# Causal attention, second pass: triangles masked by GpSimd zero writes in place of TensorE mask products

## What is computed

```
q, k, v = proj(Wq), proj(Wk), proj(Wv)
sim = einsum('bhid,bhjd->bhij', q, k) / sqrt(hd)
sim = where(triu(ones((n, n)), k=1), neg, sim)
beta = function of the entropy of softmax(sim), one number per row
attn = softmax(sim * beta)
out = einsum('bhij,bhjd->bhid', attn, v) @ Wo.T + bo
```

## Time and profile before

| | us |
|---|---|
| median of 3 runs | 2211.95 (2209.3 to 2216.09) |
| profiled execution, its own time | 2228.5 |
| its span in the trace | 2226.7 |
| PE, DVE, ACT, POOL busy in it | 1622.6, 1482.7, 1396.0, 141.3 |
| mean granted TensorE clock | 0.753 |

### The profile page before, as it was taken

The page is one execution under the profiler, slowest core; times in us unless marked ns, Lnnn a source line. Parts: engine busy times, 40 slices in busy tenths (PEclk is TensorE's granted clock), DMA queues, the critical chain, the costliest instruction groups (busy, mean ns, idle before and its releaser), DMA issues. The chain is left out here.

```text
span 2226.7 us, 22386 instructions
## 1 busy us (share of the span) xinstructions
PE 1622.6 (73%) x6402; PEld 690.0 (31%) x6402; DVE 1482.7 (67%) x3509; ACT 1396.0 (63%) x2635; POOL 141.3 (6%) x126
## 2 busy tenths in 40 slices
PE   4786899999999643777778787788787877511166
PEld 2343344444444201232223332232222333201144
DVE  6645354535463799888887788877878763479922
ACT  4464443434333598989989999899999986300012
POOL 0000000000000100000000000000000000035364
PEclk9898899999999755676765667656655578755578
DMA  4000065554556201111111011110101002240031
GB/s 147 0 0 0 16 160 156 132 155 128 158 147 168 68 34 33 55 47 61 38 47 46 29 58 41 44 46 31 58 29 37 36 24 87 58 123 0 0 104 48
DMA packets 56668, 147.37 MB, mean 66 GB/s; under 512 B 7760, under 2 KB 22480, under 8 KB 53936
## 3 DMA queue, kind: packets, MB, share of 16 engines
q1 hardware_dynamic: 52320, 136.63, 20.6%
q0 software_dynamic: 3072, 8.39, 1.3%
q10 hardware_dynamic: 1152, 0.92, 0.3%
HBM read 126.38 MB, written 19.53 MB: 66 GB/s over the span
## 5 line engine op out<-in xcount | busy, mean ns | idle before, releaser
L1712 DVE CUSTOM_DVE_ANT_0 sa_e<-sa_ps,sa_mask 128x1024 f32<-128x1024 f32 (+7 forms) x512 | 385.9, 754 | 107.0 <-PE sa_ps L1459 101.5
L1459 PE MATMUL sa_ps<-sa_space 72*128 72x512 bf16 (+3 forms) x768 | 296.9, 456 | 188.2 <-DVE sa_nmax L1712 140.1
L1721 DVE CUSTOM_DVE_ANT_0 sa_lg<-sa_e,sa_lg 128x1024 f32<-128x1024 f32 (+7 forms) x512 | 386.4, 755 | 67.3 <-ACT sa_lg L1612 67.0
L1602 ACT ACTIVATE sa_e<-sa_e,sa_nmax 128x1024 f32<-128x1024 f32 (+7 forms) x512 | 406.6, 794 | 20.1 <-DVE sa_nmax L1712 19.4
L1612 ACT ACTIVATE sa_lg<-sa_e,sa_sum 128x1024 f32<-128x1024 f32 (+7 forms) x512 | 405.5, 792 | 5.0 <-DVE sa_prod L1721 4.7
L1620 ACT ACTIVATE sa_p<-sa_ps 128x512 f32<-128x512 f32 x576 | 338.4, 610 | 71.6 <-PE sa_ps L1509 40.7
L1509 PE MATMUL sa_ps<-sa_q2s,sa_k2s 75*128 75x512 bf16 (+3 forms) x768 | 297.7, 432 | 50.1 <-ACT sa_p L1620 35.9
L974 DVE TENSOR_TENSOR mx_hw<-mx_spread,mx_h 128x512 f32<-128x512 f32 x256 | 176.1, 691 | 232.2 <-PE mx_ps L813 197.1
L875 ACT ACTIVATE mx_h<-mx_ps 128x512 f32<-128x512 f32 (+1 forms) x264 | 157.0, 597 | 276.6 <-PE mx_ps L800 256.0
L800 PE MATMUL mx_ps<-mx_f,m 128*128 128x512 f32 x512 | 261.4, 596 | 0.8 <-ACT mx_h L875 0.8
L813 PE MATMUL mx_ps<-mx_hw,m 128*128 128x512 f32 x512 | 259.8, 594 | 1.0 <-DVE mx_hw L974 1.0
(11 more groups left out here) (322 smaller groups left out, 1846.2 us busy)
## 6 DMA issues: line engine op xcount, KB each, us to landing
mx_spread<-mx_spill SPq DMA_DIRECT2D x256, 256.0 KB, 4.0
sa_space<-sa_spill_q SPq DMA_DIRECT2D x96, 96.0 KB
sa_space<-sa_spill_k SPq DMA_DIRECT2D x96, 96.0 KB
sa_k2s<-sa_spill_k SPq DMA_DIRECT2D x48, 192.0 KB
sa_q2s<-sa_spill_q SPq DMA_DIRECT2D x48, 192.0 KB
m<-m_in SPq DMA_DIRECT2D x1, 4256.0 KB, 18.5
records<-sa_e SPq DMA_DIRECT2D x8, 512.0 KB, 5.3
be_w<-w_in SPq DMA_DIRECT2D x16, 256.0 KB, 11.4
```

Of the source, the lines that this page charges most:

```text
L1459: last = nc.tensor.matmul(out[:, col:col + w], q_ring[:, c % 2, local, i * P:(i + 1) * P], k_ring[:, c % 2, local, col:col + w], start=Tru ...
L1602: nc.scalar.activation(e[:, u % 5, 0:w], e[:, u % 5, 0:w], ACT.Exp, scale=-1.0, bias=nmax[:, b % 2, i, h:h + 1], accum_out=sums[:, b % 2, ...
L1712: nc.vector.tensor_tensor_reduce(out=e[:, u % 5, 0:w], in0=slot_of("unit", u)[:, 0:w], in1=mask_wide[:, SEQ - w:SEQ], scale=1.0, scalar=3. ...
L1721: nc.vector.tensor_tensor_reduce(out=lg[:, u % 2, 0:w], in0=e[:, u % 5, 0:w], in1=lg[:, u % 2, 0:w], scale=1.0, scalar=0.0, op0=ALU.mult, ...
```

## The change

The mask products of the second pass (L1512) are left out: PE computes the diagonal blocks unmasked, and ACT exponentiates them as they are. POOL then goes through the packs: for each diagonal block it waits until all four exponentials of the pack are done, and one `affine_select` over 128 partitions x 4 heads x 128 columns of fp32 in `p_t`, in place, keeps an element where column >= partition and writes 0.0 elsewhere. `answer(v)` gets one more wait, on POOL's count up to and including pack v. There is one `affine_select` for a single pack and two for a double pack, 128 in all, and 512 fewer products on PE. The mask of the first pass (`mask_wide`) stays.

```diff
+        def own_cols(s):
+            return [sum(w for _, _, w in PACKS[s][:k]) for k, (j, q, _) in enumerate(PACKS[s]) if q == j * P]
+
+        def own_blocks(v):
+            g, s = divmod(v, NPACKS)
+            return TILES * g + sum(len(own_cols(k)) for k in range(s))
+
+        masked = sig("sa_masked")
+
...
             def _(pool):
                 pool.wait_ge(mask_ready.sem, 2)
                 nc.gpsimd.memset(k2_ring[64:ROWS2, :, :, :], 1.0).then_inc(ready.sem, 1)
+                for v in range(ALL2):
+                    for col in own_cols(v % NPACKS):
+                        pool.wait_ge(exp2_ready.sem, GROUP * (v + 1))
+                        whole = p_t[:, v % 2, :, col:col + P]
+                        nc.gpsimd.affine_select(out=whole, in_=whole, pattern=[[0, GROUP], [1, P]], compare_op=ALU.is_ge,
+                                                fill=0.0, base=0, channel_multiplier=-1
+                                                ).then_inc(masked.sem, 1)
...
                     for j, q, w in PACKS[s]:
-                        own = q == j * P
                         last = nc.tensor.matmul(out[:, col:col + w], k2_ring[:, g % 2, hh, j * P:(j + 1) * P],
-                                                q2_ring[:, g % 2, hh, q:q + w], start=True, stop=not own)
-                        if own:
-                            last = nc.tensor.matmul(out[:, col:col + P], ident_b[:, :], mask_k,
-                                                    start=False, stop=True)
+                                                q2_ring[:, g % 2, hh, q:q + w], start=True, stop=True)
                         col += w
                     last.then_inc(s2_mm.sem, 1)
...
                     pe.wait_ge(exp2_ready.sem, GROUP * (v + 1))
+                    if own_blocks(v + 1):
+                        pe.wait_ge(masked.sem, own_blocks(v + 1))
```

## The result

The changed kernel takes 2223.46 us (median of 7 runs, 2218.88 to 2228.5) against 2212.38 for the kernel before (7 runs, 2206.95 to 2217.06) beside it: a ratio of 1.0052, 95% interval 1.004 to 1.0065. It is slower by 11 us. The profiled execution took 2223.03 us, with a span of 2221.3 and a mean granted clock of 0.735.

A forecast was written before the change was run, and what follows sets the result against it. ACT was taken to set the main stage's pace, with PE leading in the tail. The terms -3 - 4 + 6 + 3 + 8 = +10 us, on the median of 2211.95, gave 2222 us; range 2200 to 2262.

The forecast's parts named there:

- Masks out, main stage and tail: PE without 512 mask products: main stage -3 us (bounds 0 and -42), tail -4 us (bounds 0 and -5).
- ACT's waits fall in packs 6 and 7: Sign to look for: ACT's waits before its second-pass exponential should fall in these packs and rise in the tail.
- Ended with a mask product: ACT's waits for PE where a mask product was the last thing awaited: 12.6 us main stage, 18.4 us tail.
- The select's duration: POOL's time per 128x512 select, taken as 1.5 us from a one-input TENSOR_SCALAR; two with hand-over 3.2 us.
- The wait in the main stage: Double packs' answers wait for POOL beyond their slack; PE late by 22 us, a quarter let through: +6 us.
- the 2.5 us of slack: Main stage: time from a double pack's last exponential to its answer, which hides POOL's selects up to that length.
- The expected 0.5 to 1 us for packs 1 and 8: Sign to look for: the answer's new wait on POOL in these main-stage packs.
- DVE and POOL side by side: Main stage: selects hold off DVE's two-input product, 13 us of DVE time, a quarter let through: +3 us.
- The tail: Answers with almost no slack wait for POOL; PE late by 16.5 us, half let through: +8 us.
- the 104 to 110 us named: Sign to look for: the tail's length after the change, instead of 101 us.
- The fast select rival: Selects below 1.15 us each, no main-stage overrun, PE relieved: -12 us, 2200 us; chance 0.20.
- The reading, 0.62 of 1.49 us: From the earlier trace: a one-input POOL operation holds DVE's two-input ones off only for its first 0.62 us.

The follow-up runs named there:

- the second measurement: The changed kernel itself, unaltered, timed once more beside the kernel before: 1.0036.
- the kernel with neither: Changed kernel without mask products, selects or the wait on POOL; triangles unmasked, second-pass exponentials at 1/128 of their scale: 0.9954 of the kernel before.
- Selects aside: Changed kernel without mask products; the 128 selects run on a tile of their own, no answer waits; exponentials at 1/128 scale: 1.0008 of the kernel before.
- memsets aside: As Selects aside, but each select is a memset of the same size, so POOL writes and reads nothing: 0.9974 of the kernel before.

## Why the prediction was right, and which step failed

The forecast was 2222 us; the median is 2223.46. The sum of +10 stands against +11 measured (1.0052; 1.0036 in the second measurement is +8), and it is made of terms that did not all hold.

- **Masks out, main stage and tail (-3 and -4).** Measured together as -10, by the kernel with neither. The bounds of 0 to -47 held it. In the last 21 packs of the tail they show as nothing (85.8 us with masks, 86.5 without), so the split into -3 and -4 isn't borne out. The expectation that ACT's waits fall in packs 6 and 7 did not come true: read from the gaps on ACT, pack 6 has 8.0 us instead of 8.4 and pack 7 has 6.6 in both. "Ended with a mask product" was no measure of what the wait would lose.
- **The select's duration (1.5 us): this is the step that failed.** A select takes 0.63 us when DVE lets it, and 0.82 on the mean, from 0.63 up to 1.62. I had taken the TENSOR_SCALAR as the nearest row because inputs and output agree. The memset at 530 ns was the nearer one.
- **The wait in the main stage (+6): nil.** With 0.63 to 0.82 us a double pack's two selects fit into the 2.5 us of slack; of 67 masked packs three answers waited, for 0.7 us in all. The expected 0.5 to 1 us for packs 1 and 8 did not come. The slack of the double packs was read rightly. That of single packs was not: 3.9 us holds for pack 0, but pack 6 has 1.2 to 2.4 us in 8 of its 13 answers. With selects of 0.63 us nothing came of it.
- **DVE and POOL side by side (+3): mis-sized.** Selects aside cost 0.54% over neither on the same chip, 12 us. The sum counted 13 us of DVE's time, a quarter of which was to reach the end; DVE's busy time grew by 4.7 us only, since `product` rose by 6 ns and not by 30. So the time held was put too high and its effect too low. The hold also goes both ways, and the sum counted one of them: POOL is held too, by 24 us in all (128 x 0.19), with single selects at up to 1.62 us.
- **The tail (+8, with -4 of masks): right in size, by another sum.** +4 forecast net, +4.9 and +4.5 in two profiles, inside the 104 to 110 us named; the last answer waited 2.24 us for POOL. Without the first two packs, where the kernel before had the lower clock by chance, it is +7.1 to +7.5. The overrun was smaller than I had summed (9.0 us against 16.5). The rest came from what I had put at 0 here: the selects' presence beside DVE and a clock of 0.83 instead of 0.86. Selects that nobody waits for cost 4 to 6 us in the last 21 packs by themselves.
- **The fast select rival.** Its condition held: less than 1.15 us each. Its price did not come, -12 us. It assumed that a fast select costs nothing beyond the wait, and that half of ACT's waits behind masks would go.

The last answer shows the tail's term by itself. Timeline after, at the end of the tail, against the earlier trace rows:

```profile
1915.74 0.57 ACT L1634 ACTIVATE sa_p<-sa_ps 128x512 f32<-128x512 f32 x1
1916.38 1.22 POOL L1431 TENSOR_SCALAR_AFFINE_SELECT sa_p<-sa_p 128x512 f32<-128x512 f32 x2 [4.23 <-ACT sa_p L1634]
1917.75 1.05 PE L1542 MATMUL sa_ps<-sa_p,sa_space 128*9 128x256 f32 x16 [2.24 <-POOL sa_p L1431]
```

From the end of the last exponential (1916.31) to the last answer it is 1.44 us, where it was 0.05: 0.07 to POOL, 1.22 for two undisturbed selects, 0.15 to PE.

The range of 2200 to 2262 held, and the largest part of the chances stood on slower. That +10 came so near was in part luck: a term too high in the main stage's wait (+6) made up for one too low in the contention (+3).

Of the Trainium skill's two rules, the GPSIMD Engine Reference (section 3.1, Elementwise) gave 769 ns for 512 elements; the trace has 0.63 alone and 0.82 on the mean, nearer to it than my 1.5. SBUF — State Buffer (Who interferes with whom) says that the later of the two blocks for the whole of the other. The trace agrees on both sides, as the rows at the end of this document show: a select that meets such an operation of DVE ends 0.49 us behind it, and one of DVE that starts within a select is held up until about the select's end. The reading, 0.62 of 1.49 us, is the one that stands apart.

Open remains what carries 7 to 12 us from the selects' presence to the end of the kernel, when DVE is busy for 4.7 us more; what lowers the clock in the tail; and how the price of the wait divides between its own 9.0 us and that clock. Another place for the selects in the main stage, such as between two `product`s, wasn't tried.

## What to carry to other kernels

Before work moves from a busy engine to an idle one, ask what the bounding engine got from it: here ACT's wait for PE in the main stage was 42 us before and 42 after. It is 33 to 41 us in the other kernels without masks there and 38 in the one with masks and selects, so what 428 products were worth to it is lost in its scatter. Work on an idle engine can have a price without any wait, as these selects had; one kernel that does the work on a tile of its own and has nobody wait for it measures that price by itself. One profile of a stage that starts at a varying clock misleads by some us; leaving the first packs out, and comparing several kernels with the same program in that stage, makes the rest plain. And look in the trace for whether an inserted product stands where it was meant to. Read the slack stage by stage: a hand-over that is free behind 2.5 us of slack costs more than its length where the slack is zero.

## What the runs showed that was not expected

- **A select is faster than simpler arithmetic.** On 128x512 fp32, from the list by line of POOL after, whole span:

```profile
L1431 POOL TENSOR_SCALAR_AFFINE_SELECT sa_p<-sa_p 128x512 f32<-128x512 f32 x128 | 103.1, 822 | 1056.6 <-ACT sa_p L1634 1056.6
...
L2094 POOL TENSOR_SCALAR as_p<-as_d 128x512 f32<-128x512 f32 x6 | 8.9, 1491 | 0.5
```

- **Of a select and a DVE operation with two SBUF inputs, the later waits for the earlier.** In the tail after, a pair of selects beside a two-input operation, and a single one beside another:

```profile
1871.32 1.23 DVE L114 TENSOR_TENSOR sa_e<-sa_cent,sa_rstd 128x1024 f32<-128x1024 f32 x1 [0.64 <-ACT sa_rstd L110]
...
1871.84 1.20 POOL L1431 TENSOR_SCALAR_AFFINE_SELECT sa_p<-sa_p 128x512 f32<-128x512 f32 x1 [17.98 <-ACT sa_p L1634]
...
1873.79 2.21 POOL L1431 TENSOR_SCALAR_AFFINE_SELECT sa_p<-sa_p 128x512 f32<-128x512 f32 x2 [0.75 <-ACT sa_p L1634]
1873.83 1.67 DVE L90 SCALAR_TENSOR_TENSOR sa_cent<-sa_sums,sa_e 128x1024 f32<-128x1024 f32 x1
```

The single select starts within L114 and takes 1.20 us instead of 0.63: it ends at 1873.04, 0.49 us behind the end of L114 at 1872.55. Of the pair, the first starts 0.04 us ahead of L90 and would end at 1874.42; L90, which takes 1.23 us elsewhere, takes 1.67, so it is held up by 0.44. The second select then starts within L90, which ends at 1875.50, and is done at 1876.00, again about 0.49 us behind it. The pair takes 2.21 instead of 1.22. The same holds over the whole pass: 48 selects start while `product` runs; they take 0.98 us on the mean, and every one of them ends 0.49 us behind that `product`. 38 start while `evacuate` runs (one input in PSUM), and none of them takes more than 0.64. Of the 62 memsets aside that start while `product` runs none takes more than 0.53. The selects lose 24 us in all and DVE's operations 5, because POOL mostly comes second: a select starts within `product` 48 times, `product` within a select 24 times.

- **More work for PE is free here.** 192 bank fills issued twice raise the granted clock of the main stage from 0.65 to 0.70, and the time is 0.9986 [0.9969, 1.0003]: neither lost nor measurably gained.
- **The profiled execution of the kernel before** stood 16 us above its median. From 1912 us on, behind attention, it has 315.7 us, and the one after 302.5, with the same code. In the twelve experiments this part is either 300.6 to 302.7 or 315.9 to 317.6 us, the same for all that ran on one chip. So it goes with the chip in these runs, and says nothing about the change.
